# A first sweep without GpSimd additions, with TensorE summing some chunks and a mixed chunk order, and the last stage's steps written as straight code with the update one slot later

## What is computed

```python
# layer 0, graph: x = x + relu(A_norm @ (layernorm(x) @ W.T))
A_hat = adj + eye
d_inv_sqrt = sum(A_hat, axis=1) ** (-0.5)
A_norm = d_inv_sqrt[:, None] * A_hat * d_inv_sqrt[None, :]
# layer 1, feed-forward: x = x + (30 times step)(layernorm(x))
def step(h):
    h = h + 0.01 * tanh(h)
    h = h * sigmoid(h)
    h = layernorm(h, ln_w, ln_b)
    return h @ W.T + b
```

## Time and profile before

| | us |
|---|---|
| median of 3 runs (lowest to highest) | 2027.58 (2027.34 to 2028.16) |
| the profiled execution | 2028.44 |
| its span in the profile | 2026.7 |
| end of panel 1 to end of panel 8 in the first sweep | 67.2 to 244.9 |
| second sweep's contractions | 244.9 to about 407 |
| the loop of steps (28 of 30 steps) | 1236.6 to 1986.4 |

### The profile page before, as it was taken

One profiled execution on the slowest core, in us unless ns is written; L12 is line 12 of the kernel. 1 busy time (PEld: TensorE's weight loads), 2 busy tenths in 40 slices (PEclk: granted clock), 3 DMA queues, 4 the chain that ended last, 5 costly groups with the idle time before them and its releaser, 6 DMA issues. The chain is left out here.

```text
span 2026.7 us, 44601 instructions
## 1 busy us (share of the span) xinstructions
PE 1816.9 (90%) x12898; PEld 1741.1 (86%) x12898; DVE 1650.8 (81%) x4233; ACT 1339.8 (66%) x2735; POOL 1035.0 (51%) x1756
## 2 busy tenths in 40 slices
PE   6468899919999999778999969999999999999998
PEld 4368899919999999767999959989998989999997
DVE  4888977738999999657666649989899989999897
ACT  4323455516666666345566649888888988889885
POOL 4543325444555555440000027777777777777774
PEclk9778999959999999988999989999999999999999
DMA  8755579427888788425666400000000000000001
GB/s 292 241 191 180 167 208 198 111 90 240 232 231 233 232 236 230 101 76 203 187 184 183 121 6 2 2 3 2 3 1 3 2 3 1 1 1 0 3 1 69
DMA packets 101001, 226.46 MB, mean 112 GB/s; under 512 B 21313, under 2 KB 51779, under 8 KB 92364
## 3 DMA queue, kind: packets, MB, share of 16 engines
q1 hardware_dynamic: 86220, 206.33, 32.7%
q0 software_dynamic: 14592, 17.91, 4.6%
HBM read 204.43 MB, written 19.75 MB: 111 GB/s over the span
## 5 line engine op out<-in xcount | busy, mean ns | idle before, releaser
L2341 PE MATMUL ffn_psH<-ffn_w2h,ffn_vTh 128*128 128x256 f32 x1320 | 406.2, 308 | 11.4 <-DVE ffn_vTl L2408 11.3
L2341 PE MATMUL ffn_psH<-ffn_w2h,ffn_vTl 128*128 128x256 f32 x1320 | 374.9, 284 | 0.0
L2341 PE MATMUL ffn_psH<-ffn_w2l,ffn_vTh 128*128 128x256 f32 x1320 | 374.0, 283 | 0.0
L2448 POOL TENSOR_SCALAR ffn_vn<-ffn_vn,ffn_rstd,ffn_shift 128x256 f32<-128x256 f32 x540 | 299.7, 560 | 20.2 <-issue 0.3
L2415 DVE SCALAR_TENSOR_TENSOR ffn_u<-ffn_th,ffn_psH 128x512 f32<-128x512 f32 x390 | 265.2, 680 | 49.2 <-ACT ffn_th L2368 49.0
L2403 DVE BATCH_NORM_STATS2 ffn_stats<-ffn_vn 128x6 f32<-128x256 f32 x780 | 281.8, 404 | 14.2 <-issue 11.9
L2341 PEld LDWEIGHTS ffn_psH<-ffn_w2h,ffn_vTh 128*128 128x128 f32 x1320 | 252.3, 191 | 35.2 <-DVE ffn_vTl L2408 18.2
L2371 ACT ACTIVATE ffn_vn<-ffn_u 128x512 f32<-128x512 f32 x390 | 254.8, 653 | 15.2 <-DVE ffn_u L2415 15.2
L2341 PEld LDWEIGHTS ffn_psH<-ffn_w2l,ffn_vTh 128*128 128x128 f32 x1320 | 253.6, 192 | 0.0
L2341 PEld LDWEIGHTS ffn_psH<-ffn_w2h,ffn_vTl 128*128 128x128 f32 x1320 | 252.7, 191 | 0.0
L2322 PE MATMUL ffn_psT<-ident,ffn_vn 128*128 128x128 f32 x1560 | 234.4, 273 | 9.1 <-POOL ffn_vn L2448 3.8
(11 more groups left out here) (244 smaller groups left out, 5205.2 us busy)
## 6 DMA issues: line engine op xcount, KB each, us to landing
g_raw<-in_adjt SPq DMA_DIRECT2D x272, 384.0 KB, 3.8
moe_w1raw<-in_wall SPq DMA_DIRECT2D x33, 1024.0 KB
moe_w2raw<-in_wall SPq DMA_DIRECT2D x33, 1024.0 KB, 5.8
g_raw<-in_adjl SPq DMA_DIRECT2D x27, 256.0 KB, 2.7
moe_b<-in_eb SPq DMA_DIRECT2D x33, 128.0 KB, 4.8
xn_rows<-rt_hn SPq DMA_DIRECT2D x8, 384.0 KB, 4.5
x_rows<-x SPq DMA_DIRECT2D x8, 384.0 KB, 6.4
out<-ffn_vn SPq DMA_DIRECT2D x12, 256.0 KB
```

What stands on the lines that cost most here:

```text
L2341: last = pe.matmul(psH[w % R][:, q * D:(q + 1) * D], a[:, w % R, q * KD + k, :], b[:, k, :], start=(k == 0 and j == 0), stop=(k == KD - 1 ...
L2448: last = pool.tensor_scalar(vn[:, t, :], vn[:, t, :], rstd[:, s:s + 1], shift[:, s:s + 1], ALU.mult, ALU.add)
```

## The change

In the first sweep GpSimd's `add_chunk` and `fold` and VectorE's `column_sum` go. TensorE sums up to three chunks of a panel (`PE_SUMS`) by products with a matrix of ones into the bank `psP`; VectorE sums all others of the panel in one PSUM accumulator, taking turns between two from panel to panel; ScalarE copies the two halves and, where there is one, a row of TensorE's sum to SBUF (`column_sum`), and TensorE's degree products take two or three terms. `sweep_order` mixes chunks that are only summed with chunks that are also contracted, and leaves the last two of the latter for the end. `degrees`, `scale_s` and `keep_part` come some chunks later in each engine's list; the steps of `invert` and the constants of GpSimd stand in a row.

In the steps the loop is replaced by straight code over all slots, `U` and all that follows it come one slot later, and TensorE turns two items in one slot and none in the next.

```diff
-        SWEEP1 = [list(range((q * PT + 1) // CT, CHUNKS)) + list(range((q * PT + 1) // CT)) for q in range(GROUPS)]
+        def sweep_order(q):
+            first = (q * PT + 1) // CT
+            late = list(range(max(first - 2, 0), first))
+            mixed = [((a + 0.5) / (CHUNKS - first), c) for a, c in enumerate(range(first, CHUNKS))]
+            mixed += [((a + 1) / (len(late) and first - 1), a) for a in range(first - len(late))]
+            return [c for _, c in sorted(mixed)] + late
+
+        SWEEP1 = [sweep_order(q) for q in range(GROUPS)]
+
+        PE_SUMS = (0, 0, 3, 3, 3, 2, 1, 1, 0)
...
-        BY_POOL = (1, 3, 5, 7, 9)
-        BY_DVE = tuple(i for i in range(CHUNKS) if i not in BY_POOL)
...
+            def column_sum(q):
+                v = width(q)
+                act.wait_ge(dve_added, dve_sum_of(q, dve_places(q)[-1]))
+                if q >= 1:
+                    act.wait_ge(deg_mm, q)
+                last = act.activation(colsum[:, :, 0:v], deg_acc[q % 2][:, :, 0:v], ACT.Copy)
+                if PE_SUMS[q]:
+                    act.wait_ge(pe_added, sum(PE_SUMS[:q + 1]))
+                    last = act.activation(rowsum[:, 0:v], psP[0:1, 0:v], ACT.Copy)
+                last.then_inc(colsum_done, 1)
...
-                    if i == 0 and q >= 2:
+                    if i == 1 and q >= 1:
+                        column_sum(q - 1)
+                    if i == 2 and q >= 2:
                         keep_part(q - 1)
...
+                if at == 1:
+                    if q >= 2:
+                        dve.wait_ge(colsum_done, q - 1)
+                    dve.tensor_tensor(to, chunk(dve_places(q)[0]), chunk(i), ALU.add).then_inc(dve_added, 1)
+                elif at > 1:
+                    dve.wait_ge(dve_added, dve_sum_of(q, i) - 1)
+                    dve.tensor_tensor(to, to, chunk(i), ALU.add).then_inc(dve_added, 1)
...
-                        if i == 2:
+                        if i == 4:
                             degrees(q - 1)
-                        if i == 6:
+                        if i == 7:
                             scale_s(q - 1)
...
-            for q in range(GROUPS):
-                for i in range(CHUNKS):
-                    if i in BY_POOL:
-                        add_chunk(q, i)
-                    if i == BY_POOL[-1]:
-                        fold(q)
-                    if i == 3 and q >= 1:
-                        invert(q - 1)
-                    if i == 5 and q == 0:
-                        layer_norm_x(2)
-                if q == 1:
-                    route_constants()
+            layer_norm_x(2)
+            route_constants()
+            for q in range(GROUPS - 1):
+                invert(q)
...
+                for a in range(CT):
+                    last = pe.matmul(psP[:, 0:v], g.ones[:], raw[:, n % RING, a * v:(a + 1) * v], start=(at == 0 and a == 0),
+                                     stop=(at == PE_SUMS[q] - 1 and a == CT - 1))
+                last.then_inc(pe_added, 1)
...
-        LOW, MM, TANH, U, SILU, STATS, SHIFT, NORM = 1, 3, 4, 4, 5, 6, 7, 9
+        LOW, MM, TANH, U, SILU, STATS, SHIFT, NORM = 1, 3, 4, 5, 6, 7, 8, 10
...
-            for n in range(2 * G):
-                slot(n, n, 0)
-            with eng.Fori(0, (STEPS - 2) // BODY) as i:
-                for k in range(BODY * G):
-                    slot(i * (BODY * G) + (2 * G + k), 2 * G + k, i)
-            for n in range(STEPS * G, END + NORM):
+            for n in range(END + NORM):
                 slot(n, n, 0)
...
+                if G <= m < END and (m - G) % 2 == 0:
+                    for w, at in ((m, n), (m + 1, n + 1)):
```

More of the change, by code:

```diff
@@ L276, in width, with pe_places, dve_places @@
             return PANEL if q < PANELS else LPANEL
-        SWEEP1 = [list(range((q * PT + 1) // CT, CHUNKS)) + list(range((q * PT + 1) // CT)) for q in range(GROUPS)]
+        def sweep_order(q):
[6 more added lines that the diff above has]
+        PE_SUMS = (0, 0, 3, 3, 3, 2, 1, 1, 0)
+        def pe_places(q):
+            only = [i for i, c in enumerate(SWEEP1[q]) if c * CT >= q * PT]
+            n = PE_SUMS[q]
+            return [only[(2 * a + 1) * len(only) // (2 * n)] for a in range(n)]
+        def dve_places(q):
+            return [i for i in range(CHUNKS) if i not in pe_places(q)]
         PIECES = ((0, PT), (PT, 4 * PT), (4 * PT, NT))
@@ L998, in _ @@
                             support(t - 1)
-            degrees(GROUPS - 1)
             for m in range(END):
+                if m == 1:
+                    degrees(GROUPS - 1)
                 if m < TURNS:
```

120 lines of the change are left out of this document (43 added, 77 removed).

## The result

The changed kernel takes 1976.05 us, median of 4 runs (1972.08 to 1977.27), beside 2027.46 for the kernel before (4 runs, 2024.71 to 2028.16): a ratio of 0.9744, interval 0.9729 to 0.976. That is 51 us less; 57 had been forecast. The profiled execution has a span of 1973.6 us where it was 2026.7, 53.1 less.

What follows compares the result with a forecast made beforehand. VectorE was taken to pace the first sweep, with TensorE bounding it after the change; in the steps TensorE was busy 732 of 749.8 us. Gains of 30 + 15 + 13 - 1 = 57 us gave 1970 us, range 1943 to 1994.

Steps and rivals of the forecast that it cites:

- Where the bound goes in the sweep: First sweep: VectorE, stretched by GpSimd's additions, sets the pace before; after the change TensorE becomes the bound, at 139.7 us.
- The sweep's size, -30: First sweep, panels 2 to 8: 139.7 us of TensorE plus 8 of waits, ending at 215 instead of 244.6, 30 us less.
- the 8 us of waits: First sweep: TensorE's waits for late splits and degree products, taken as 8 us for all seven panels.
- The walked panels: First sweep: panels 2, 4 and 7 followed through by price, giving 15.8, 20.6 and 26.5 us.
- Rival (b): First sweep, panels 2 to 4: TensorE stays at the lower clock, costing 24 us, so 1994; chance 0.1.
- Straight code, -15: Steps: straight code has no ends of rounds, six at 2.5 us each, so 15 us less.
- Rival (c): Steps: straight code waits for its code in as many places as the loop, the 15 us stay, 1985; chance 0.08.
- The later update, -13: Steps: update one slot later; part of VectorE's wait for tanh goes, 0.46 us a step, 13 us less over 28 steps.
- rival (a): Steps: the wait on tanh goes whole and TensorE sets the pace, 37 us instead of 13, 1946; chance 0.2.
- four such waits: Steps: VectorE's waits for ScalarE's tanh, four in two steps, each losing 0.23 us, so 0.46 a step.
- Pairing, forecast at nothing: Steps: turning two groups together saves TensorE nothing; the second of a pair needs its normalised rows one slot earlier.
- rival (d): Steps: a group's ring becomes too long, 2.2 us missing a step, 62 us lost, 2046; chance 0.05.

## Why the prediction was right, and where its sizes were not

**Where the bound goes in the sweep: right.** VectorE's two groups fell to their undisturbed prices, TensorE became the bound, and GpSimd's additions are shown to be the cause of the stretching by putting them back. Two other edits of the sweep are not needed for it: without sums on TensorE the sweep took 148.3 us, in the old chunk order 155.3; the later places of the degrees, the scaling and the copy were not tried alone. One detail was wrong: the prediction held that operations with two inputs in SBUF are stretched. The scaling `g_sh` has one large input, and it went from 0.87 to 4.86 us. What went undisturbed were the additions that read and write PSUM beside one input in SBUF. The Trainium skill ("SBUF — State Buffer", Who interferes with whom) says that VectorE and GpSimd share one pair of SBUF ports, and that this pair is what contends; the rows agree, and the size (5.6 times for `g_sh`, 3.4 for `g_sl`) is theirs alone.

**The sweep's size, -30: 10 us too much.** The term that failed is TensorE's work, which was priced at full clock throughout. The sum has 133.0 us of work (139.7 less the stops) and 14.7 of stops and waits (6.7 and 8). In the changed kernel TensorE stands only 10.1 us, so the 8 us of waits were not too few; but it is busy 147.9. With both disturbances taken away, at a clock of 1.00, it is busy 137.3 and stands 8.9. That the sweep then took 146.1, within 2 us of the 147.7 forecast, is in part luck: work 4 us dearer and waits 6 us cheaper than reckoned. The walked panels were near: 15.8, 20.6 and 26.5 us for panels 2, 4 and 7, and 14.9, 20.1 and 26.9 in that kernel.

What the sum put at nothing was the lower clock, 0.50 for 23.9 us of the changed sweep, and two things brought most of it. First, panel 3's chunks come late behind the four transfers of constants: 5.1 us, 2.2 of them standing and the rest work at the lower clock behind the wait. The prediction had reckoned DMA by its mean share of 0.75 and found it hidden; a mean share does not show the 2.5 us in which it is under 0.3. In the trace before, the same four transfers stand ahead of panel 3's chunks as well, and VectorE waits 3.0 us for chunks there; whether for this reason was not tested in that kernel, but the rows were there to be read:

```profile
88.56 0.97 DVE L558 TENSOR_TENSOR g_psT<-g_raw 128x768 f32<-128x768 f32 x1 [2.00 <-DMA g_raw<-in_adjt]
92.46 2.54 DVE L558 TENSOR_TENSOR g_acc<-g_raw 128x768 f32<-128x768 f32 x1 [1.00 <-DMA g_raw<-in_adjt]
```

Second, the degree products: behind 18 one-column records in a row the clock falls in most of the late panels, for 1.5 us each time. Spreading them removed 5.9 us in panels 5 to 8. The prediction had priced them at their own length (2.2 us, measured 2.6 from 127.69 to 130.32) and nothing more.

**Rival (b), the lower clock: it came in half its size, and only partly for its reason.** (b) had panels 2 to 4 at 1.2 GHz throughout, at a cost of 24 us; here 23.9 us passed at that level, which costs about half as much. Of these 10.2 lie in panels 2 and 3, behind waits of 1.94 and 3.42 us, which is the idle time that (b) speaks of; the other 13.7 lie in panels 5 to 8, where TensorE has no idle time but 0.9 us at each panel's start. So what was given a chance of 0.1 accounts for the missing 10 us (147.9 us of busy time against 137.3 at full clock). Nor was the argument against it, "with tiles and summed chunks mixed it has work from 67 us on", what kept the clock up elsewhere: the old order ran at 0.95 and no slower than the mixed one.

**Straight code, -15: right.** 749.0 to 734.9 is 14.0 without the other edits, 732.4 to 718.2 is 14.2 with them. Rival (c), that straight code would wait for its code elsewhere, fell. The Trainium skill ("Runtime: NRT & Kernel Launch", Instruction fetch mechanics) says that a branch breaks the sequential fetching of code; that agrees with 2.3 to 2.4 us for each of the six ends, though no row here shows the fetch itself.

**The later update, -13: right in kind, too small.** The waits did not vanish, which was rival (a), but moved from the update to the statistics that need the same SiLU: 22.8 us left of 40.5 with single turns, where the prediction's rule (0.98 a step) gave 27. The mis-sized term is "four such waits" that lose 0.23 us each. In two steps there were 1.14, 0.60, 0.60 and 0.50 us, and 0.90, 0.37 and 0.36 are left: the longest lost 0.24, as the prediction worked out, and three of the four are still there, but the fourth is gone whole, and why that one was not followed up. So 40.5 - 22.8 = 17.7 us are 0.63 a step, not 0.46. With single turns the steps gained 734.9 - 715.0 = 19.9 us.

**Pairing, forecast at nothing: it costs 3 us.** The prediction named the reason, that the second item of a pair needs its normalised rows a slot earlier, priced it in rival (d) alone and put it at nothing in its sum. The rows show 8.6 us of waits before TensorE's turns, nearly all for GpSimd, against 1.7. So the 31.7 us are 14.0 + 19.9 - 3.2, and 0.9 by which the loop itself differed between two kernels that have it alike (749.9 and 749.0). Rival (d), the same ring too long by 2.2 us a step, was not near: the waits are 0.3 us a step. Its sign, waits of TensorE for normalised rows that grow, did show in small: 3.8 us in the loop before, 8.3 after.

In sum, a sweep 10 us worse and steps 4 us better than forecast, with 2.6 us from stretches for which no gain was forecast, gave 53 us in the trace where 57 had been expected. That the whole came as near as this owes something to misses of opposite sign. The low end of the range, 1943, does not follow from the terms named for it: by the prediction's own sum 44 in the sweep gives 1956 and 37 in the steps 1946.

## What to carry to other kernels

When the bound passes to another engine, price the new engine's waits from events, not from mean shares: look at what stands in the DMA queue just ahead of its inputs, and price its work at the clock that it will have, not at the full one alone: here the clock fell behind waits and behind a row of tiny products. A wait that hangs on one event moves to the next instruction that needs the same event: reckon what is left there for each of the waits and not from the longest alone. And take a change apart before keeping all of it; here the chunk order gave nothing, and the paired turns and the late panels' sums cost. Without these two, and with the constants late and the degrees spread, the kernel ran 21 us faster.
